# The last FFN block's output: residual rows written first, scaled result added by an accumulating scatter

## The chip, the cores and the metric

The kernel runs on one core of a Trainium2 chip. The metric is device time of one execution in microseconds (us). The engines named below are PE (TensorE, matmuls), DVE (VectorE), ACT (ScalarE), POOL (GpSimd, which also issues the indirect DMAs) and SP (SyncE, which issues the plain DMAs).

## What is computed

The reference, cut to what matters. `x` has 4 x 512 = 2048 tokens of 512 numbers; `L0_xattn_ref` sends each token through one of four gated products with the context of its expert, and `L0_ffn_ref` is a gated FFN with 1408 inner columns.

```python
def _L0_ffn_ref(x, gate_w, up_w, down_w, gate_s, up_s, down_s):
    g = jnp.einsum('th,ih->ti', xf, gate_w) * gate_s
    u = jnp.einsum('th,ih->ti', xf, up_w) * up_s
    hdn = jax.nn.silu(g) * u
    out = jnp.einsum('ti,hi->th', hdn, down_w) * down_s
...
x = x + jnp.tanh(g_xattn[0]) * _L0_xattn_ref(_layernorm(x, axis=-1), itok_BxS_13_99985, ctx_2048, ctx_2048, ctx_2048)
x = x + jnp.tanh(g_ffn[0]) * _L0_ffn_ref(_layernorm(x, axis=-1), L0_ffn_gate_w, L0_ffn_up_w, L0_ffn_down_w, L0_ffn_gate_s, L0_ffn_up_s, L0_ffn_down_s)
```

So each output row is x1 (the row after the first of these two updates) plus `tanh(g_ffn) * down_s` times the row of the down product.

## The kernel before, in words

The first part (up to about 170 us) sorts the tokens by expert, gathers their rows, computes the expert update and stores the updated rows x1 in a scratch tensor `x1_rows` in HBM (`x_rows` in the profile's names). The second part, `second_mlp`, is the FFN. It takes the 16 tiles of 128 tokens in four blocks (`b` = 0 to 3) of four tiles. In a block it goes through 11 chunks `c` of 128 inner columns: gate product and up product (L1032), SiLU on ACT (L511), product with the up part on DVE (L807), a split of the result into a high part (ACT, L515) and a low part (DVE, L812), and then the down product (L1045) into four PSUM banks `acc_ps[0..3]`, one for each tile `u` of the block. The down product of chunk c-1 runs behind the gate and up products of chunk c, and the last chunk of a block behind the first gate and up products of the next. For the last block nothing comes behind: its chunk 10 is cut in two halves of 256 columns (`halves`), and when it is done the program's last part begins.

A block is finished by `finish(b)` on DVE. For each pair of tiles it runs `scale` twice (L834: `tmp` or `xn` = `acc_ps[u]` times `dsb`, where `dsb` holds `tanh(g_ffn) * down_s`) and `add` twice (L841: `rows` = `rows` + `tmp` or `xn`, where `rows` holds x1). Each `add` raises the semaphore `rows_ready`. For blocks 0 to 2 it stands inside the next block's first chunk; `finish(3)` is the last thing on DVE.

POOL scatters each finished tile to `out` with an indirect DMA (L442), whose destination rows are in `oidx`. Tile u of PSUM is tile t = (u + 2) mod 4 of the block. In blocks 0 to 2 each scatter waits for the one before it to land (`out_stored`); the last four don't wait for each other and have a semaphore each (`last_stored[t]`). The order on every engine is the order of the program's text.

SP loads a block's x1 rows by two plain DMAs (`load_rows`, L304, semaphores `rows_a` and `rows_b`), for block 3 once eight scatters have landed. `rows` has eight slots of 512 numbers, four for each of two blocks. At the end SP waits for the four `last_stored` (L324), and each engine ends with a DRAIN and a semaphore exchange (L76, the end of the block of programs).

Of the kernel before, what the change touches and what calls it, by code (L numbers as in the profile page):

```python
# [18 lines left out]
ALU = mybir.AluOpType  # L19
# [11 lines left out]
STEPS = TILES + EXPERTS - 1  # L31
# [3 lines left out]
BLOCK = 4  # L35
BLOCKS = TILES // BLOCK
# [22 lines left out]
def row_slot(b, t):  # L59

    return (RING + BLOCK * b + t) % ROWS
# [7 lines left out]
def build(nc, x, ids, ctxT, g_x, g_f, guT, dwT, gate_s, up_s, down_s, out):  # L69
# [6 lines left out]
    with ExitStack() as ctx:  # L76
        def sb(name, shape, dt):
            return ctx.enter_context(nc.sbuf_tensor(name, shape, dt))
# [4 lines left out]
        def sem(name):  # L83
            return ctx.enter_context(nc.semaphore(name))
# [9 lines left out]
        rows = sb("rows", [P, ROWS, D], F32)  # L94
# [3 lines left out]
        dsb = sb("dsb", [P, D], F32)  # L98
# [15 lines left out]
        oidx = sb("oidx", [P, TILES], U32)  # L114
# [71 lines left out]
        acc_ps = bank[2:6]  # L186
# [40 lines left out]
        S = {n: sem(n) for n in names}  # L227
        ctx_landed = [sem(f"ctx_landed{e}") for e in range(EXPERTS)]
        down_landed = [sem(f"down_landed{n}") for n in range(4)]
        last_stored = [sem(f"last_stored{t}") for t in range(BLOCK)]  # L230

        def hold(eng):

            eng.sem_inc(S["held"])
# [92 lines left out]
        def _(pool):  # L327
# [32 lines left out]
            def inverse_std(m):  # L360
                pool.wait_ge(S["var_ready"], m + 1)
                pool.tensor_tensor(rstd[:, 0:1], ve[:, 0:1], half[:, :], ALU.pow)\  # L362
                    .then_inc(S["rstd_ready"], 1)
# [62 lines left out]

            pool.wait_ge(S["oidx_ready"], 1)

            for b in range(BLOCKS):
                if b + 1 < BLOCKS:  # L430
                    for t in range(BLOCK):
                        inverse_std(STEPS + BLOCK * (b + 1) + t)
                for u in range(BLOCK):
                    n, t = BLOCK * b + u, (u + 2) % BLOCK
                    pool.wait_ge(S["rows_ready"], STEPS + n + 1)
                    if b + 1 < BLOCKS:
                        if n:
                            pool.wait_ge(S["out_stored"], 16 * n)
                        done = S["out_stored"]
                    else:  # L440
                        done = last_stored[t]
                    pool.indirect_dma_start(  # L442
                        out, bass.IndirectOffsetOnAxis(ap=oidx[:, BLOCK * b + t:BLOCK * b + t + 1], axis=0),
                        rows[:, row_slot(b, t), :], None).then_inc(done, 16)

        @block.scalar
        def _(act):
# [86 lines left out]
        def _(dve):  # L534
# [292 lines left out]
            def scale(b, u):  # L827

                n = BLOCK * b + u
                buf = (tmp, xn)[u % 2]  # L830
                dve.wait_ge(S["acc_done"], n + 1)
                if u >= 2:
                    dve.wait_ge(S["rows_ready"], STEPS + n - 1)
                dve.tensor_tensor(buf[:, :].unsqueeze(1), acc_ps[u][:, :].unsqueeze(1),  # L834
                                  dsb[:, :].unsqueeze(1), ALU.mult).then_inc(S["scaled"], 1)

            def add(b, u):

                at = row_slot(b, (u + 2) % BLOCK)
                dve.wait_ge(S["scaled"], BLOCK * (b + 1) + u + 1)  # L840
                dve.tensor_tensor(rows[:, ds(at, 1), :], rows[:, ds(at, 1), :],  # L841
                                  (tmp, xn)[u % 2][:, :].unsqueeze(1), ALU.add)\
                   .then_inc(S["rows_ready"], 1)

            def finish(b):

                dve.wait_ge(S["dsb_ready"], 1)
                dve.wait_ge(S["rows_ready"], STEPS + BLOCK * b)
                for u in range(0, BLOCK, 2):
                    scale(b, u)  # L850
                    scale(b, u + 1)
                    add(b, u)
                    add(b, u + 1)

            def mlp_block(b, first=False, last=False):
                for c in range(IC):
                    chunk(b, c)
                    if first:
                        for d in range(3 * c, min(3 * c + 3, IC)):
                            down_lo(d)  # L860
                    if first and c == IC - 1:
                        dve.tensor_scalar(dsb[:, :], dsb[:, :], tg[:, 1:2], None, ALU.mult)\
                           .then_inc(S["dsb_ready"], 1)
                    if c == 0 and not first:
                        dve.wait_ge(S["xt_done"], STEPS + BLOCK * (b + 1))
                        finish(b - 1)
                    if c - 1 in PREP_AT and not last:
                        t = PREP_AT[c - 1]
                        x_lo(STEPS + BLOCK * (b + 1) + t, b + 1, (t + 2) % BLOCK)
                    if c in PREP_AT and not last:  # L870
                        if PREP_AT[c] == 0:
                            dve.wait_ge(S["rows_ready"], STEPS + BLOCK * b)
                        prepare(b + 1, PREP_AT[c])
# [4 lines left out]
            with dve.Fori(1, BLOCKS - 1) as b:  # L878
                mlp_block(b)
            mlp_block(BLOCKS - 1, last=True)  # L880
            finish(BLOCKS - 1)

        @block.tensor
        def _(pe):
# [225 lines left out]
```

## Time and profile before

| | us |
|---|---|
| median of 3 runs | 424.78 |
| lowest, highest | 424.2, 425.44 |
| span of the profiled execution (first to last instruction) | 422.8 |
| PE busy in the span | 373.6 (88%) |
| DVE busy | 249.7 (59%) |
| ACT busy | 139.7 (33%) |
| POOL busy | 98.6 (23%) |

The page's times are positions in the profiled span of 422.8 us, counted from its first instruction. The median of the runs, 424.78 us, is 2.0 us more than that span, which is what lies around the first and the last instruction. "L442" is a line of the kernel before. A name such as POOLq or DVEq is an engine's sequencer, which takes the waits, the DRAINs and the semaphore exchanges.

### The profile page before, as it was taken

How to read it: one execution, taken by the hardware profiler on the slowest of the kernel's cores; microseconds unless marked ns; L12 is line 12 of the kernel's file. 1: busy time of each engine (PE TensorE's matmuls, PEld its weight loads, DVE VectorE, ACT ScalarE, POOL GpSimd, SP SyncE). 2: the span in 40 equal slices, each digit the busy share in tenths (PEclk: the TensorE clock that was granted, in tenths of full speed). 3: DMA queues.
4: the chain of work that ended last, by engine and by line, in shares of the span. 5: the costliest groups of instructions: out<-in, count | busy, mean ns of one | idle time of the engine just before them, and what ended most of it. 6: DMA issues, size and time to landing. Idle time of an engine off the chain costs nothing.

```text
span 422.8 us, 6048 instructions
## 1 busy us (share of the span) xinstructions
PE 373.6 (88%) x1740; PEld 305.6 (72%) x1740; DVE 249.7 (59%) x461; ACT 139.7 (33%) x240; POOL 98.6 (23%) x135
## 2 busy tenths in 40 slices
PE   0117999999999984999999999999999999999990
PEld 0015788888778863888888888788888888888870
DVE  6998888888878782654653624654524645422243
ACT  4502545454545331542232222322222222222220
POOL 4553455554553221000000200100200100200003
PEclk9999999999999996999999999999999999999996
DMA  7445455655532043422000140000130000100002
GB/s 266 152 131 161 135 160 179 203 154 175 164 133 99 25 149 102 123 70 85 2 0 0 50 149 0 1 0 0 74 124 0 0 0 0 74 25 0 0 1 99
DMA packets 14956, 34.52 MB, mean 82 GB/s; under 512 B 2400, under 2 KB 2400, under 8 KB 14944
## 3 DMA queue, kind: packets, MB, share of 16 engines
q1 hardware_dynamic: 10624, 20.21, 15.1%
q0 software_dynamic: 4320, 14.16, 9.7%
q8 instruction: 6, 0.10, 0.1%
q14 instruction: 6, 0.05, 0.0%
HBM read 25.19 MB, written 9.18 MB: 81 GB/s over the span
## 4 chain that ended last, share of the span: by engine, by line
PE 84%; DVE 9%; issue 2%; POOL 2%; DMA 1%; POOLq 0%; ACT 0%; DVEq 0%
PE bank L1032 38%; PE bank L922 22%; PE bank L1045 19%; PE bank L914 3%; PE bank L936 2%; DVE work L239 1%; DMA rows<-x,gidx 1%; DVE shifted L625 1%; POOL out L442 1%; DVE work L677 1%; DVE is_low L607 1%; POOL rstd L362 1%; DVE is_low L633 1%; DMA ids_i<-ids 0%; DVE is_high L602 0%
## 5 line engine op out<-in xcount | busy, mean ns | idle before, releaser
L1032 PE MATMUL bank<-work,wgu 128*128 x704 | 169.4, 394 | 5.3 <-issue 5.3
L1032 PEld LDWEIGHTS bank<-work,wgu 128*128 128x128 f32 x704 | 133.9, 190 | 33.8 <-issue 5.5
L922 PE MATMUL bank<-work 128*128 x432 | 109.8, 403 | 3.6 <-DVE work L677 2.9
L922 PEld LDWEIGHTS bank<-work 128*128 128x128 f32 x432 | 79.7, 190 | 21.0 <-issue 5.2
L807 DVE SCALAR_TENSOR_TENSOR sh<-bank,gs,sh 128x512 f32<-128x512 f32 (+1 forms) x45 | 33.1, 738 | 96.9 <-PE bank L1032 96.8
L1045 PE MATMUL bank<-work,hp 128*128 128x512 f32 x352 | 88.2, 393 | 0.0
L1045 PEld LDWEIGHTS bank<-work,hp 128*128 128x128 f32 x352 | 65.1, 188 | 13.2 <-DVE hp L812 0.2
L511 ACT ACTIVATE sh<-bank,gs 128x512 f32<-128x512 f32 x44 | 30.3, 689 | 91.4 <-PE bank L1032 90.6
L515 ACT ACTIVATE hp<-sh 128x512 fp32r<-128x512 f32 (+1 forms) x45 | 28.0, 623 | 89.0 <-DVE sh L807 89.0
L362 POOL TENSOR_TENSOR rstd<-ve,half 128x1 f32<-128x1 f32 x31 | 17.9, 577 | 136.3 <-DVE ve L644 136.3
L812 DVE TENSOR_TENSOR hp<-sh,hp 128x512 fp32r<-128x512 f32 (+1 forms) x45 | 30.6, 681 | 30.1 <-ACT hp L515 30.0
L442 POOL DMA_INDIRECT out<-rows,oidx x16 | 16.3, 1022 | 117.6 <-DVE rows L841 94.0
L677 DVE TENSOR_TENSOR work<-bank,work 128x512 fp32r<-128x512 f32 (+1 forms) x35 | 23.8, 684 | 1.3 <-issue 1.0
L650 DVE TENSOR_SCALAR xn<-rows,mv,rstd 128x512 f32 (+1 forms) x31 | 16.9, 544 | 10.4 <-POOL rstd L362 10.4
L469 ACT ACTIVATE sh<-bank 128x512 f32<-128x512 f32 x19 | 11.4, 599 | 35.1 <-PE bank L922 35.1
L461 ACT ACTIVATE work<-bank 128x512 fp32r<-128x512 f32 (+1 forms) x35 | 20.4, 590 | 5.5 <-PE bank L904 3.8
L639 DVE BATCH_NORM_STATS2 bn<-rows 128x6 f32 (+1 forms) x31 | 21.2, 684 | 0.0
L914 PE MATMUL bank<-ident,xn 128*128 128x128 f32 x124 | 19.2, 278 | 2.0 <-issue 1.7
L914 PEld LDWEIGHTS bank<-ident,xn 128*128 128x128 f32 x124 | 15.3, 142 | 6.8 <-issue 2.4
L696 DVE SCALAR_TENSOR_TENSOR rows<-bank,tg,rows 128x512 f32 (+1 forms) x19 | 14.2, 749 | 8.3 <-PE bank L922 8.2
L703 DVE TENSOR_TENSOR wgu<-raw,wgu x16 | 14.3, 893 | 7.2 <-issue 7.2
L465 ACT ACTIVATE work<-bank 128x512 fp32r<-128x512 f32 x18 | 10.8, 600 | 18.1 <-PE bank L936 18.1
(125 smaller groups left out, 251.3 us busy)
## 6 DMA issues: line engine op xcount, KB each, us to landing
raw<-guT SPq DMA_DIRECT2D x16, 352.0 KB
ctx_in<-ctxT SPq DMA_DIRECT2D x4, 1024.0 KB, 9.1
rows<-x_rows SPq DMA_DIRECT2D x8, 512.0 KB, 4.2
checked<-dwT SPq DMA_DIRECT2D x11, 256.0 KB, 3.1
rows<-dwT SPq DMA_DIRECT2D x11, 256.0 KB, 2.7
dsb<-down_s SPq DMA_DIRECT2D x1, 256.0 KB, 5.2
out<-rows,oidx POOLq DMA_INDIRECT x16, 2.7
rows<-x,inow POOLq DMA_INDIRECT x12, 3.5
```

The source lines that it names most:

```text
L362: pool.tensor_tensor(rstd[:, 0:1], ve[:, 0:1], half[:, :], ALU.pow)\
L442: pool.indirect_dma_start(out, bass.IndirectOffsetOnAxis(ap=oidx[:, BLOCK * b + t:BLOCK * b + t + 1], axis=0), rows[:, row_slot(b, t), :], ...
L511: act.activation(sh[:, :], g_ps[:, :], ACT.Silu, scale=gs[:, 0, c:c + 1])\
L515: act.activation(hslot(c)[:, 0, part], sh[:, part], ACT.Copy)\
L639: dve.bn_stats(bn[:, 0, :], rows[:, ds(at, 1), :]).then_inc(S["bn_parts"], 1)
L677: dve.tensor_tensor(xpart(b, u, 1), turned[:, :], xpart(b, u, 0).bitcast(F32), ALU.subtract)\
L807: dve.scalar_tensor_tensor(out=sh[:, part], in0=u_ps[:, part], scalar=gs[:, 1, c:c + 1], in1=sh[:, part], op0=ALU.mult, op1=ALU.mult).then ...
L812: dve.tensor_tensor(hslot(c)[:, 1, part], sh[:, part], hslot(c)[:, 0, part].bitcast(F32), ALU.subtract)\
L914: mm = pe.transpose(xt_ps[:, c * P:(c + 1) * P], xn[:, c * P:(c + 1) * P], ident[:, :])
L922: mm = pe.matmul(out_ps[:, :], part(s)[:, c * P:(c + 1) * P], ctx_w(e, c, w), start=n == 0, stop=n == last)
L1032: mm = pe.matmul(out_ps[:, :], wgu[:, row + h, w, c * P:(c + 1) * P], moving, start=n == 0, stop=n == last)
L1045: mm = pe.matmul(acc_ps[u][:, :], hslot(c)[:, s, u * P:(u + 1) * P], down_w(c, w), start=c == 0 and n == 0, stop=c == IC - 1 and n == len( ...
```

## The change

For the last block alone, POOL now writes the block's x1 rows to `out` as soon as the block's x1 loads have landed and POOL is through with the scatters of block 2; each of these four scatters raises its own semaphore `x1_out[t]`. `finish(3)` is gone from DVE. In its place stand four multiplications of `acc_ps[u]` by `dsb`, which write straight into the slot of `rows` that held x1, after the scatter that reads that slot has landed (`x1_out[t]`). POOL then issues four scatters to the same rows of `out` with `compute_op=ALU.add`, each after the multiplication (`scaled`) and after the landing of the x1 row it adds to. Blocks 0 to 2 are as they were.

```diff
+        x1_out = [sem(f"x1_out{t}") for t in range(BLOCK)]
...
-            for b in range(BLOCKS):
-                if b + 1 < BLOCKS:
-                    for t in range(BLOCK):
-                        inverse_std(STEPS + BLOCK * (b + 1) + t)
+            def out_rows(b, t):
+                return bass.IndirectOffsetOnAxis(ap=oidx[:, BLOCK * b + t:BLOCK * b + t + 1], axis=0)
+
+            for b in range(BLOCKS - 1):
+                for t in range(BLOCK):
+                    inverse_std(STEPS + BLOCK * (b + 1) + t)
                 for u in range(BLOCK):
                     n, t = BLOCK * b + u, (u + 2) % BLOCK
                     pool.wait_ge(S["rows_ready"], STEPS + n + 1)
-                    if b + 1 < BLOCKS:
-                        if n:
-                            pool.wait_ge(S["out_stored"], 16 * n)
-                        done = S["out_stored"]
-                    else:
-                        done = last_stored[t]
-                    pool.indirect_dma_start(
-                        out, bass.IndirectOffsetOnAxis(ap=oidx[:, BLOCK * b + t:BLOCK * b + t + 1], axis=0),
-                        rows[:, row_slot(b, t), :], None).then_inc(done, 16)
+                    if n:
+                        pool.wait_ge(S["out_stored"], 16 * n)
+                    pool.indirect_dma_start(out, out_rows(b, t), rows[:, row_slot(b, t), :], None)\
+                        .then_inc(S["out_stored"], 16)
+
+            b = BLOCKS - 1
+            pool.wait_ge(S["rows_a"], 16 * BLOCKS)
+            pool.wait_ge(S["rows_b"], 16 * BLOCKS)
+            for t in range(BLOCK):
+                pool.indirect_dma_start(out, out_rows(b, t), rows[:, row_slot(b, t), :], None)\
+                    .then_inc(x1_out[t], 16)
+            for u in range(BLOCK):
+                t = (u + 2) % BLOCK
+                pool.wait_ge(S["scaled"], BLOCK * (b + 1) + u + 1)
+                pool.wait_ge(x1_out[t], 16)
+                pool.indirect_dma_start(out, out_rows(b, t), rows[:, row_slot(b, t), :], None,
+                                        compute_op=ALU.add).then_inc(last_stored[t], 16)
...
-            finish(BLOCKS - 1)
+
+            for u in range(BLOCK):
+                t = (u + 2) % BLOCK
+                dve.wait_ge(S["acc_done"], BLOCK * (BLOCKS - 1) + u + 1)
+                dve.wait_ge(x1_out[t], 16)
+                dve.tensor_tensor(rows[:, row_slot(BLOCKS - 1, t), :], acc_ps[u][:, :], dsb[:, :], ALU.mult)\
+                   .then_inc(S["scaled"], 1)
```

DVE at the very end of the program, before (numbers behind `bank` and `hp` are left out; L834 is `scale`, L841 is `add`):

```order
L812 TENSOR_TENSOR hp_51<-sh,hp_51 128x256 [waits hhi_ready] x2
L834 TENSOR_TENSOR tmp<-bank,dsb 128x512 [waits acc_done,rows_ready,dsb_ready]
L834 TENSOR_TENSOR xn<-bank,dsb 128x512 [waits acc_done]
L841 TENSOR_TENSOR rows<-rows,tmp 128x512 [waits scaled]
L841 TENSOR_TENSOR rows<-rows,xn 128x512 [waits scaled]
L834 TENSOR_TENSOR tmp<-bank,dsb 128x512 [waits rows_ready,acc_done]
L834 TENSOR_TENSOR xn<-bank,dsb 128x512 [waits rows_ready,acc_done]
L841 TENSOR_TENSOR rows<-rows,tmp 128x512 [waits scaled]
L841 TENSOR_TENSOR rows<-rows,xn 128x512 [waits scaled]
```

The same place after (L823 is the line that was L812):

```order
L823 TENSOR_TENSOR hp_51<-sh,hp_51 128x256 [waits hhi_ready] x2
L897 TENSOR_TENSOR rows<-bank,dsb 128x512 [waits x1_out2,acc_done]
L897 TENSOR_TENSOR rows<-bank,dsb 128x512 [waits x1_out3,acc_done]
L897 TENSOR_TENSOR rows<-bank,dsb 128x512 [waits x1_out0,acc_done]
L897 TENSOR_TENSOR rows<-bank,dsb 128x512 [waits x1_out1,acc_done]
```

Eight instructions became four, and the tile that is scattered first is written by the first of them instead of the third.

POOL at the end of the program, before, from the last `rstd` of block 3 on (the first four scatters are block 2's, the last four block 3's):

```order
L362 TENSOR_TENSOR rstd<-ve,half 128x1 [waits var_ready] x4
L442 DMA out<-rows,oidx 2048x512 [waits out_stored,rows_ready] x4
L442 DMA out<-rows,oidx 2048x512 [waits rows_ready] x4
L76 UNCONDITIONAL_BRANCH
```

The same place after:

```order
L363 TENSOR_TENSOR rstd<-ve,half 128x1 [waits var_ready] x4
L441 DMA out<-rows,oidx 2048x512 [waits out_stored,rows_ready] x4
L448 DMA out<-rows,oidx 2048x512 [waits rows_b,rows_a]
L448 DMA out<-rows,oidx 2048x512 x3
L454 DMA out<-rows,oidx 2048x512 [waits x1_out2,scaled]
L454 DMA out<-rows,oidx 2048x512 [waits x1_out3,scaled]
L454 DMA out<-rows,oidx 2048x512 [waits x1_out0,scaled]
L454 DMA out<-rows,oidx 2048x512 [waits x1_out1,scaled]
L76 UNCONDITIONAL_BRANCH
```

Four scatters (L448) were put between block 2's and the last four, and the last four (L454) are of the accumulating kind and wait for two things each.

## Rows read from the trace of the kernel before

**Rows 1.** The page: busy tenths of PE, granted clock, by slices of 10.6 us

```profile
PE   0117999999999984999999999999999999999990
...
PEclk9999999999999996999999999999999999999996
```

**Rows 2.** Chain that ended last, in order of time: start, us, what

```profile
411.01 0.69 DVE tmp L834
411.70 0.60 DVE xn L834
412.30 0.61 DVE rows L841
412.91 0.27 issue
413.18 1.16 POOL out L442
414.33 0.30 issue
...
416.86 1.26 POOLq L76
```

**Rows 3.** Timeline of the end: start, us, engine, line, what, idle before

```profile
411.62 0.68 DVE L834 TENSOR_TENSOR xn<-bank,dsb 128x512 f32<-128x512 f32 x1
412.22 0.68 DVE L841 TENSOR_TENSOR rows<-rows,tmp 128x512 f32<-128x512 f32 x1
...
415.29 0.68 DVE L841 TENSOR_TENSOR rows<-rows,xn 128x512 f32<-128x512 f32 x1
...
417.17 0.96 POOL L442 DMA_INDIRECT out<-rows,oidx  x1 [0.30 <-issue]
```

**Rows 4.** Line L76, the program's end, by engine: duration in ns, start

```profile
L76 POOLq DRAIN  x1: 6609/6609/6609, 416.0 to 416.0; - x1
L76 SPq DRAIN  x1: 7/7/7, 420.2 to 420.2; - x1
L76 SPq EVENT_SEMAPHORE  x1: 17/17/17, 422.8 to 422.8; - x1
...
L76 DVEq DRAIN  x1: 1270/1270/1270, 414.7 to 414.7; - x1
```

**Rows 5.** Line L442, the last four scatters (from 400 us on): ns, landing

```profile
L442 POOL DMA_INDIRECT out<-rows,oidx x4: 956/960/1159, 413.2 to 417.2; - x4
...
DMA to landing us min/median/max: 2.7/2.7/2.9
```

**Rows 6.** DMA queues, 412 to 423 us, in 40 slices of 0.275 us: busy tenths

```profile
DMA  0000000000599009950399108970000000000000
...
q0 software_dynamic: 320, 1.05, 25.0%
```

**Rows 7.** Line L351, the gathers from HBM by POOL: ns, landing

```profile
L351 POOL DMA_INDIRECT rows<-x,inow x12: 1013/1023/1030, 53.6 to 125.8; - x12
...
DMA to landing us min/median/max: 3.3/3.6/5.3
```

**Rows 8.** Timeline around block 2's scatters and behind them

```profile
366.62 0.69 DVE L812 TENSOR_TENSOR hp<-sh,hp 128x512 fp32r<-128x512 f32 x1 [0.70 <-ACT hp L515]
...
369.23 0.96 POOL L442 DMA_INDIRECT out<-rows,oidx  x1 [2.53 <-DMA out<-rows,oidx]
...
372.07 0.69 DVE L812 TENSOR_TENSOR hp<-sh,hp 128x512 fp32r<-128x512 f32 x1 [0.70 <-ACT hp L515]
```

**Rows 9.** Busy time by stretch: us, PE, PEld, DVE, ACT, POOL, clock, DMA

```profile
358.00:372.00 14.00, 14.00 (x64) 11.58 (x63) 6.78 (x11) 3.79 (x6) 4.10 (x4) 1.00 0.20 75
372.00:382.00 10.00, 10.00 (x46) 8.29 (x45) 2.64 (x4) 2.05 (x4) 0.00 (x0) 1.00 0.00 0
```

**Rows 10.** Timeline of SP from 300 us on: block 3's x1 loads

```profile
310.11 0.87 SPq L304 DMA_DIRECT2D rows<-x_rows  x2
```

## The prediction

> **What bounds the kernel now.** I read the page's busy tenths first: PE is at 9 in nearly every slice from the fifth to the last but one, at full granted clock but for one slice ahead of the FFN (around 165 us) [rows 1]. So during the FFN blocks anything that DVE, POOL or the DMA engines do beside PE is free as long as PE gets its operands in time, and only the last slice is open to this change. Then the chain of waits in order of time [rows 2]: up to 411.0 us it is matmuls; from there it runs over two `scale` on DVE, one `add`, 0.27 us of semaphore and start, and then POOL's four scatters back to back. After that the timeline of the same stretch [rows 3] and the program's end by engine [rows 4].
>
> The end has two stretches. The first is DVE from the last accumulation to the first row ready for POOL: 411.01 to 412.91, three steps of 0.60 to 0.69 us. The second is POOL: its first scatter starts at 413.18 and takes 1.16 us, the others 0.96 with 0.30 between them, so the last starts at 417.17 and ends at 418.13 [rows 2, 3, 5]. DVE is through with its last `add` at 415.97 [rows 3], 1.2 us before POOL takes that tile: **from the first scatter on, POOL's issue rate sets the pace, not DVE**. The data follow: each scatter shows as a burst of about 3 slices of 0.275 us with gaps between the bursts, and the last burst ends near 419.4 [rows 6]; landed is 2.7 us after the start of the issue, 419.87 [rows 3, 5]. SP is released then and is at its own DRAIN at 420.2. But the span ends at 422.8, and what ends just before is POOL's DRAIN: 416.0 + 6.61 = 422.6 [rows 4]. That is 4.5 us after POOL's last issue and 2.7 us after the last landing; the DVE's DRAIN, 414.7 + 1.27 = 415.97, ends exactly with its last instruction [rows 3, 4]. **What POOL's DRAIN waits for, the issue or the landing, this trace doesn't tell**, since there is one such DRAIN in it. That is the choice on which the forecast hangs most.
>
> **The change part by part.**
>
> *Four x1 scatters on POOL, early.* They stand behind block 2's last scatter, which ends at 370.19 [rows 8]. Their waits on `rows_a` and `rows_b` are long met: SP issued block 3's loads at 310.1 to 311.0 [rows 10]. So they run from about 370.5 on, 4 x 0.96 + 0.2 + 3 x 0.30 = 4.9 us, to about 375.5, and land by 378. Nothing stands behind them on POOL until 411.7, and SP waits only for the last four. The work that hides them is PE's: between 358 and 372 us PE was busy 14.00 of 14.00 us with four such scatters beside it (4.10 us of POOL, DMA share 0.20), as it was between 372 and 382 without any [rows 9]. DVE's `hp` subtraction took 0.69 us beside and without a scatter [rows 8]. Cost: 0. If the cover were not there they would cost 4.9 us of POOL, which is why they have to be before 411.
>
> *DVE's new waits on `x1_out`.* They are met 33 us before `acc_done`. Queued behind them are only the four multiplications themselves. Cost: one more semaphore check, under 0.05 us on the first.
>
> *DVE's `add` gone.* The row that POOL takes first is ready when the first multiplication ends. Before, that took two `scale` and one `add` (0.69 + 0.60 + 0.61 us); now it takes one instruction of 0.69 us, ending at 411.70. The gain is 412.91 - 411.70 = **1.21 us** on the chain. The other three follow at 0.60 us each (412.3, 412.9, 413.5), faster than POOL takes them, so the four further instructions that fall away bring nothing. POOL's first scatter starts at 411.70 + 0.27 + 0.01 = 411.98 instead of 413.18.
>
> *The accumulating scatter, issue.* No row shows one. Its nearest row is the plain scatter of the same tile, 0.96 us [rows 5], and that is the lower end: the same 128 indices and the same two tensors. An upper end is twice that, 1.92, if reading the old row of `out` costs POOL as much again as the whole plain issue. Between them the plain gather with 1.02 us [rows 7] shows how far POOL's indirect issues spread by form. I take 1.02, near the plain row, because the list of indices is read once either way, and add nothing for the second wait, which is met when its turn comes. Then the last issue ends at 411.98 + 0.20 (the first one's excess) + 4 x 1.02 + 3 x 0.30 = 417.16, against 418.13: **-0.97 us**. At 0.96 it is -1.20, at 1.44 (half as much again) it is 418.84, or +0.7, at 1.92 it is +2.6. The two break even at 1.26 us an issue.
>
> *The accumulating scatter, data.* It reads the tile, reads the old rows of `out` and writes them. The plain one has the DMA engines for about 0.69 us (a quarter of 11 us for four, [rows 6]) of the 1.27 us between issues; twice that, 1.4 us, is a little more than the interval, and would queue 0.1 us on each. The read also comes ahead of the write in time. Gathers from HBM landed after 3.3 to 5.3 us, scatters after 2.7 [rows 5, 7]. With 0.6 to 2.6 us more than 2.7, the last landing is 411.98 + 0.20 + 3 x 1.32 + 3.3 to 5.3 = 419.4 to 421.4, against 419.87. I take the lower third of it, 419.9, since the gathers' 5.3 was beside other traffic and here there is none: the shift of 0.97 is eaten, and **the last row lands when it does now**. SP has 2.6 us from its DRAIN to the end of the span [rows 4], so up to about 422 this is hidden, if POOL's DRAIN doesn't wait for it.
>
> The page "Collectives: The Full Stack" of the Trainium skill (The bandwidth ceiling) speaks against this part: a reduce in the DMA engines needs two source reads for each chunk, both on one ring, and runs at half the rate of a copy. By it the scatter's 0.69 us would be 1.4, which the sum above has already as its bound; nothing in this case's trace shows an accumulating DMA to agree or differ.
>
> *Sum.* Issue -0.97, landing hidden: span 422.8 - 0.97 = 421.8, and with the 2.0 us around it 423.8.
>
> **The rivals.**
>
> A, the forecast: POOL's DRAIN follows its last issue by 4.5 us. 423.8, from 423.6 (0.96 us an issue) to 424.3 (1.15).
>
> B, the gain is handed back by the landing: POOL's DRAIN waits until the DMAs have landed and adds its 2.7 us. Then the end moves with the landing, 419.4 to 421.4 against 419.87: -0.5 to +1.5, likeliest near 0 to +0.3: 424.9. For it: the DRAIN is the only one that outlasts its engine's last instruction, and only POOL has DMAs of this kind out. Against it: 2.7 us after a landing is long for an engine that is merely told of it, when SP gets from its wait to its DRAIN in 0.3.
>
> C, the other side: accumulating issues are dearer than POOL's pace allows. The chain is POOL's four issues, so each extra 0.1 us costs 0.4. The place is the last 6 us; it is slower than now from 1.26 us an issue, and by over 1.27 us (0.3%) from 1.58. At 1.44 it gives 425.5. For it: three addresses a row instead of two. Against it: gathers and scatters of different form lie within 0.06 us of each other.
>
> D, the DMA engines add slowly: three times the copy's 0.69 us and more. Then the bursts join, 4 x 2.1 us from the first data at about 413.5, the last row lands at about 422.3 and SP's part ends the span near 422.8 if the DRAIN doesn't wait (424.8), or near 425.2 if it does (427.2).
>
> **How the numbers follow.** Chances: A 0.45, B 0.26, C 0.18, D 0.11. The likeliest is A, so the predicted time is 423.8. The range takes in A and B whole and C up to 1.6 us an issue, and leaves out D with the DRAIN waiting and a dearer C: 423.2 to 426.2, which also allows for the 0.5 us by which single runs stand apart. A measurement of this kernel tells about 0.3%, 1.27 us, from no change; faster by that means below 423.51, which A reaches only at its lower end and with luck: 0.14. Slower by that means above 426.05: half of D, a third of C, a quarter of B: 0.05 + 0.07 + 0.07, and a little for what I have not thought of: 0.22. The rest, 0.64, is within 0.3%.
>
> **What would show each step.** In the profile after: the first multiplication at 411.0 and the first accumulating scatter at 412.0 (if later, the waits on `x1_out` cost). The duration of the last four scatters: about 1.0 us is A or B, 1.3 or more is C. Four plain scatters near 370.5 to 375.5 with PE still fully busy in 372 to 382. Time to landing of the last four: 2.7 to 3.7 is the sum, above 5 with bursts that touch each other is D. The end of POOL's DRAIN against the last issue and the last landing: 4.5 us after the issue is A, 2.7 after the landing B. The prediction fails if the issue or the landing of an accumulating scatter lies outside the bounds taken, or if DRAIN has a cost of its own with such DMAs.

## The result and the profile after

The changed kernel takes 427.86 us (median of 4 runs, 427.26 to 427.92) against 424.49 us for the kernel before beside it: ratio 1.0073, 95% interval 1.0059 to 1.0087. By the ratio it is 3.1 us slower, where 1 us less was forecast, and it lies outside the range of 423.2 to 426.2. The profiled execution has a span of 425.7 us, 2.9 more than before.

Line numbers of the changed kernel: L897 is the last multiplication on DVE, L448 the early scatter, L454 the accumulating scatter, L1062 the down product. Up to the end of PE's work nothing differs. This is busy time by stretch, with the columns of [rows 9], for the changed kernel:

```profile
358.00:372.00 14.00, 14.00 (x63) 11.59 (x63) 6.72 (x11) 3.76 (x6) 5.37 (x6) 1.00 0.20 77
372.00:382.00 10.00, 10.00 (x46) 8.29 (x45) 2.70 (x4) 2.01 (x3) 2.57 (x3) 1.00 0.27 102
```

PE is as full as in [rows 9] with the four early scatters beside it. The end, from the timeline of the changed kernel, answers to [rows 2, 3]:

```profile
410.86 2.48 DVE L897 TENSOR_TENSOR rows<-bank,dsb 128x512 f32<-128x512 f32 x4 [0.45 <-PE bank L1062]
411.83 1.60 POOL L454 DMA_INDIRECT out<-rows,oidx  x1 [36.65 <-DVE rows L897]
413.73 1.58 POOL L454 DMA_INDIRECT out<-rows,oidx  x1 [0.30 <-issue]
...
417.48 1.55 POOL L454 DMA_INDIRECT out<-rows,oidx  x1 [0.31 <-issue]
```

POOL starts 1.35 us earlier than before (411.83 against 413.18); 0.15 of it is PE, which ended that much earlier in this execution, and 1.20 is the change, as the sum had it. But each issue takes 1.57 us instead of 0.96, so the last one ends at 419.03 instead of 418.13. The lines of the accumulating scatter (L454), of the DMA queues from 412 to 426 us in 40 slices of 0.35 us, and of the program's end (L76) answer to [rows 5], [rows 6] and [rows 4]:

```profile
L454 POOL DMA_INDIRECT out<-rows,oidx x4: 1551/1568/1597, 411.8 to 417.5; - x4
...
DMA to landing us min/median/max: 5.0/5.4/5.6
```

```profile
DMA  0000099959699899998999998996200000000000
...
q0 software_dynamic: 576, 1.05, 56.3%
```

```profile
L76 POOLq DRAIN  x1: 12082/12082/12082, 413.4 to 413.4; - x1
...
L76 SPq DRAIN  x1: 7/7/7, 423.4 to 423.4; - x1
```

Landing takes 5.0 to 5.6 us instead of 2.7. The bursts that stood apart in [rows 6] have run together, from 413.8 to about 422. The same 1.05 MB went in 576 packets instead of 320, and the DMA engines were busy for 0.563 x 14 = 7.9 us, 1.97 a scatter, instead of 0.69. The last row lands at 423.1, SP is at its DRAIN at 423.4, and POOL's DRAIN ends at 413.4 + 12.1 = 425.5, 2.4 us after the last landing and 6.5 after POOL's last issue. Before, it was 2.7 and 4.5. Neither of the two distances that the forecast chose between was kept, so what that DRAIN does had to be found out.

### The profile page after: what moved, and what is told of

The parts are those of the page before. It is cut to its first block, busy times and chain, and to the rows that moved or that the text cites. A ratio compares the mean times of both kernels' runs of the same rounds, so it can differ in the third digit from the quotient of the medians.

```text
span 425.7 us, 6054 instructions
## 1 busy us (share of the span) xinstructions
PE 374.5 (88%) x1740; PEld 306.8 (72%) x1740; DVE 247.5 (58%) x457; ACT 139.6 (33%) x240; POOL 104.5 (25%) x139
## 4 chain that ended last, share of the span: by engine, by line
PE 72%; issue 12%; DVE 9%; DMA 3%; POOL 2%; ACT 1%; POOLq 0%; DVEq 0%
PE bank L1049 30%; PE bank L939 23%; PE bank L1062 14%; PE bank L931 3%; DMA out<-rows,oidx 3%; PE bank L953 2%; DVE work L240 1%; DVE shifted L636 1%; POOL out L454 1%; DVE work L688 1%; DVE is_low L618 1%; DVE is_low L644 1%; POOL out L448 0%; POOLq L76 0%; DMA ids_i<-ids 0%
## 5 line engine op out<-in xcount | busy, mean ns | idle before, releaser
L1062 PE MATMUL bank<-work,hp 128*128 128x512 f32 x352 | 88.2, 393 | 0.0
L1062 PEld LDWEIGHTS bank<-work,hp 128*128 128x128 f32 x352 | 65.1, 188 | 13.2 <-DVE hp L823 0.2
L823 DVE TENSOR_TENSOR hp<-sh,hp 128x512 fp32r<-128x512 f32 (+1 forms) x45 | 30.6, 680 | 30.1 <-ACT hp L526 30.0
L441 POOL DMA_INDIRECT out<-rows,oidx x12 | 12.3, 1025 | 73.7 <-DVE rows L852 51.0
L476 ACT ACTIVATE work<-bank 128x512 fp32r<-128x512 f32 x18 | 10.8, 599 | 17.9 <-PE bank L953 17.9
```

Source lines behind the costliest of these rows:

```text
L823: dve.tensor_tensor(hslot(c)[:, 1, part], sh[:, part], hslot(c)[:, 0, part].bitcast(F32), ALU.subtract)\
L1062: mm = pe.matmul(acc_ps[u][:, :], hslot(c)[:, s, u * P:(u + 1) * P], down_w(c, w), start=c == 0 and n == 0, stop=c == IC - 1 and n == len( ...
```

## The experiments

All are timed beside the kernel before. The ratio given is the one that its interval belongs to; the quotient of the two medians differs from it by up to 0.1%. The start of the tail moves by up to 1.5 us between profiled executions (the first multiplication lies at 409.9 to 411.4 us), so positions at the end are compared by their distances, not as they stand.

One thing has to be kept in mind for the comparisons with the kernel before. Its second plain scatter starts within 0.05 us of a DVE `add`. In the profiled executions of the kernel before and of e10_drain_mid its issue took 0.96 us, in those of e2_early, e3_pool_tail, e5_early_acc and e9_twelve_early 1.48 to 1.49 (the rows are in the last section). So 0.53 us of the end can come or go without any of the edits; how often it does in the runs that were only timed isn't known.

**e1_plain: the changed kernel without the adding.** The last four scatters overwrite the x1 rows, so this kernel leaves out the x1 term in the last block.

```diff
-                pool.indirect_dma_start(out, out_rows(b, t), rows[:, row_slot(b, t), :], None,
-                                        compute_op=ALU.add).then_inc(last_stored[t], 16)
+                pool.indirect_dma_start(out, out_rows(b, t), rows[:, row_slot(b, t), :], None)\
+                    .then_inc(last_stored[t], 16)
```

> The changed kernel with compute_op=ALU.add taken from the last four scatters: they overwrite the x1 rows with the scaled result instead of adding to them, so this kernel leaves out the x1 term in the last block's rows. Everything else of the change stays (early x1 scatters, four multiplications, waits). Theory 1 (the loss lies in the accumulating scatters alone: 1.57 us an issue instead of 0.96, 1.9 us of the DMA engines instead of 0.68, landing after 5.4 us instead of 2.7): the rest of the change is worth what the sum gave, -1.2 us against the kernel before, so about 423.3 us, ratio 0.997. Rival (the early scatters or the new waits cost something that the profile hides): 424.5 us or more. The last four issues take 0.96 us in theory 1.

Measured: 423.14 us against 424.83, ratio 0.9962 (0.9946 to 0.9978). The line of its last four scatters:

```profile
L454 POOL DMA_INDIRECT out<-rows,oidx x4: 957/960/961, 412.1 to 415.9; - x4
...
DMA to landing us min/median/max: 2.7/2.7/2.7
```

With `compute_op` gone the issue is back at 0.96 and the landing at 2.7. So both prices belong to the accumulating scatter. The rest of the change brings 1.6 us by the ratio, 0.9 to 2.3 by the interval, and 1.0 in the profiled execution from the first multiplication to the end of the span (421.9 - 411.13 = 10.8, before 422.8 - 411.01 = 11.8). The forecast 1.2 lies within. The 1.0 is made up of 1.2 for the earlier start, 0.2 for the first issue, which took 0.96 instead of 1.16, and 0.3 lost behind the last issue: POOL's DRAIN ends 4.8 us after it instead of 4.5. The accumulating form costs the difference between this and the changed kernel, 1.1% or some 4 to 5 us.

**e2_early and e5_early_acc: the early scatters alone.** Both are the kernel before with four scatters of block 3's x1 rows behind block 2's, and the last four waiting for them. In e5_early_acc the early ones are accumulating and wait for each other; what they add is overwritten by the last four.

```diff
+                if b == BLOCKS - 1:
...
+                    for t in range(BLOCK):
+                        pool.indirect_dma_start(
+                            out, bass.IndirectOffsetOnAxis(ap=oidx[:, BLOCK * b + t:BLOCK * b + t + 1], axis=0),
+                            rows[:, row_slot(b, t), :], None).then_inc(x1_out[t], 16)
...
```

> The kernel before with the four early x1 scatters alone added (plain, behind block 2's scatters; the last four wait for them, the final add stays on DVE). Theory 1: no difference, ratio 1.000 within 0.2%, PE fully busy in 372 to 382 us. Rival (extra DMA traffic and POOL work beside PE costs): 0.5 to 1.5 us more.

> As e2_early, but the four early scatters are accumulating ones, each waiting for the one before it to land; what they add is overwritten by the last four. Measures an accumulating scatter by itself, beside PE and off the path. Issue 1.57 us each. If its landing of 5.0 to 5.6 us in the changed kernel was its own (reading and adding), it is about 5.0 here too; if it was queueing behind its neighbours, nearer to 3.5. Time of the kernel: as before, 424.5, since all is over by about 395 us.

Measured: e2_early 1.0013 (1.0000 to 1.0026), e5_early_acc 1.0021 (1.0008 to 1.0034). PE is full in both. The first is on the edge of no difference, the second some 0.9 us slower although its early scatters are over 20 us before the end; its end resembles e2_early's, and the two intervals overlap. From the first multiplication to the end of the span e2_early's profiled execution takes 0.86 us more than that of the kernel before (12.69 against 11.83): 0.53 of it is the second issue's 1.49 us, and 0.33 a longer distance from POOL's last issue to the end of its DRAIN. The line of the early accumulating scatters of e5_early_acc, one at a time beside PE:

```profile
L441 POOL DMA_INDIRECT out<-rows,oidx x4: 1962/2005/2046, 371.5 to 387.9; - x4
...
DMA to landing us min/median/max: 5.1/5.2/5.3
```

So most of the slow landing is an accumulating scatter's own, 5.1 to 5.3 us with no neighbour; e4_acc_first has 4.5 and e8_acc_last 4.8. These figures count from the start of the issue, and here the issue took 2.0 us, since each began 0.10 to 0.16 us after a DVE subtraction of two SBUF tiles (last section). From the end of the issue it is 2.9 to 3.4 us for the ones without an accumulating neighbour (e4_acc_first, e8_acc_last and e5_early_acc) and 3.4, 3.8, 3.8 and 4.0 for the changed kernel's four. So some 0.6 to 1.1 us of the last one's landing come from its neighbours. About 0.3 of it is queueing that the rows account for (1.97 us of data at intervals of 1.88 us, three times over); the rest stays open.

**e3_pool_tail: 2.1 us more of POOL work behind the last scatter, in the kernel before.**

```diff
+            for tile in (tmp, xn, sh):
+                pool.memset(tile[:, :], 0.0)
+            pool.memset(raw[:, RAWS - 1, :], 0.0)
```

> The kernel before with about 2.4 us of memsets on POOL (three tiles of 512 and one of 704 columns) put behind its last scatter, where nobody waits for them. They end near 420.5 us, after the last landing (419.9) and before the end of POOL's DRAIN now (422.6). If the DRAIN follows POOL's last instruction by a fixed 4.5 us (forecast A): the end moves by 2.4 us to about 426.9, ratio 1.0055. If it is tied to the landing of the DMAs (rival B): no change, 424.5, ratio 1.000.

Measured: 427.0 us, ratio 1.0049 (1.0034 to 1.0065), which is the 2.1 us that the memsets took (2.4 had been planned), as a DRAIN that follows POOL's last instruction expects. The end in its timeline:

```profile
418.12 0.96 POOL L442 DMA_INDIRECT out<-rows,oidx  x1 [0.30 <-issue]
...
420.47 0.70 POOL L447 MEMSET raw<- 128x704 f32 x1
```

And the end of its program (L76):

```profile
L76 POOLq DRAIN  x1: 9291/9291/9291, 416.4 to 416.4; - x1
```

The last memset ends at 421.17, the DRAIN at 425.7: 4.5 us again, though the last row had landed at 420.8. So in the kernel before, too, it isn't the landing that sets the end.

**e7_after_tail: the same memsets behind the changed kernel's last scatter.** The edit is the one above.

> The changed kernel whole, with 2.4 us of memsets on POOL behind its last accumulating scatter, as in e3. POOL's last instruction ends near 421.4 instead of 419.0. If the DRAIN behind accumulating scatters follows POOL's last instruction by a fixed 6.45 us: +2.4 us on the changed kernel, about 430.3, ratio to the kernel before 1.013. If it is the later of two, 4.5 to 4.9 us after POOL's last instruction and 2.4 us after the last landing (423.1): the landing had set the end, and only 0.5 to 0.8 us are added, about 428.5, ratio 1.009.

Measured: 427.97 us, ratio 1.0074 (1.0056 to 1.0092), no slower than the changed kernel within the interval; a fixed distance behind POOL's last instruction would have given 430.3. The last memset in its timeline, and then its line L76:

```profile
419.96 1.28 POOL L458 MEMSET raw<- 128x704 f32 x1
```

The program's end:

```profile
L76 POOLq DRAIN  x1: 12207/12207/12207, 413.8 to 413.8; - x1
```

POOL ends at 421.24 instead of 419.03, the DRAIN at 426.0 instead of 425.5. It now comes 4.8 us after POOL's last instruction. So 1.7 of the 2.2 us were hidden: in the changed kernel the DRAIN's end is set by the landing, and its issues alone would have given 419.03 + 4.8 = 423.8.

**e8_acc_last and e4_acc_first: one accumulating scatter.** In e8_acc_last only the last of the four tiles is added by the scatter, in e4_acc_first only the first; the other three go through DVE's `add` (in e4_acc_first in the order scale, add). From the diff of e8_acc_last, POOL's part:

```diff
...
+                    if n == TILES - 1:
+                        pool.wait_ge(x1_out, 16)
+                        pool.indirect_dma_start(
+                            out, bass.IndirectOffsetOnAxis(ap=oidx[:, BLOCK * b + t:BLOCK * b + t + 1], axis=0),
+                            rows[:, row_slot(b, t), :], None, compute_op=ALU.add).then_inc(done, 16)
+                        continue
...
```

> The kernel before with only the last tile added by an accumulating scatter (its x1 rows written early); three plain issues in front as before. The last issue starts at 417.2, takes 1.6 us to 418.8, and lands 5.2 us after its start, 422.4. If the end follows the issue by 4.5 to 4.9 us: 423.3 to 423.7, +0.7 to +1.1 us, about 425.5, ratio 1.002. If it follows the landing by 2.4 us: 424.8, +2.0 us, about 426.7, ratio 1.005.

> The changed kernel with only the first tile of the last block added by an accumulating scatter (and written early); the other three go as in the kernel before, scale, add, plain scatter, in turn. POOL starts at 412.0 instead of 413.2, takes 1.57 us and then three times 0.96: the last issue starts near 416.4 against 417.17. The accumulating scatter's slow landing (5.2 us, so 417.2) lies beside the other issues. Both theories of the end (DRAIN after the last issue, or after the last landing) expect -0.5 to -0.8 us: 424.0 to 424.3 us, ratio 0.9985. If each accumulating scatter makes the DRAIN longer by its own (0.4 us each in the changed kernel), 0.4 us less of a gain.

Measured: e8_acc_last 1.0032 (1.0017 to 1.0047), e4_acc_first 0.9989 (0.9973 to 1.0005). In e8_acc_last the DRAIN ends 2.3 us after the last landing and 5.5 after the issue. Its timeline has the issue:

```profile
416.98 1.60 POOL L450 DMA_INDIRECT out<-rows,oidx  x1 [0.30 <-issue]
```

and its line L76 the end:

```profile
L76 POOLq DRAIN  x1: 8897/8897/8897, 415.2 to 415.2; - x1
...
L76 SPq COMPARE_BRANCH  x1: 43/43/43, 422.0 to 422.0; - x1
```

The last landing releases SP just ahead of that branch, at 421.8; the DRAIN ends at 424.1. The landing sets the end, and one slow scatter in the last place is enough to lose. In the first place its landing is covered by the three issues behind it. Its issue is 0.44 us longer than the kernel before's first, and the issue behind it took 1.32 us instead of 0.96, beside a DVE `add` that had begun 0.23 us ahead of it; together that is less than the 1.2 us by which POOL starts earlier. The gain isn't clear of the interval.

**e6_in_turn: no new kind of DMA, only the order of the last finish.** This is the kernel before with `finish(BLOCKS - 1, in_turn=True)`:

```diff
...
+                if in_turn:
+                    for u in range(BLOCK):
+                        scale(b, u)
+                        add(b, u)
+                    return
...
```

> The kernel before, with no accumulating and no early scatter; only the order in the last finish on DVE is changed: scale, add, scale, add, so that the first tile is ready after two instructions instead of three. The first scatter starts 0.5 us earlier, POOL's issues set the pace of the rest, and the DRAIN follows the last one by 4.5 us: -0.5 us, 424.3 us, ratio 0.999. Rival: the add waits for its own scale's result and the pair takes longer than 1.4 us, so nothing is gained.

Measured: 423.75 us, ratio 0.9986 (0.9973 to 0.9998). DVE, from its timeline:

```profile
410.21 0.69 DVE L834 TENSOR_TENSOR tmp<-bank,dsb 128x512 f32<-128x512 f32 x1 [0.55 <-PE bank L1050]
410.94 0.69 DVE L841 TENSOR_TENSOR rows<-rows,tmp 128x512 f32<-128x512 f32 x1
```

An `add` directly behind its own `scale` starts 0.73 us after it, where instructions that don't wait for each other start 0.60 apart. So the first row is ready 1.42 us after the start of the first `scale` (411.63) instead of 1.90. POOL's last issue comes 0.5 us nearer to the first multiplication (6.64 against 7.12 us), and the ratio says 0.6 us, 0.1 to 1.1 by the interval. So some 0.5 us of the changed kernel's aim of 1.2 is had without touching a DMA.

**e9_twelve_early: does the DRAIN count DMAs?** Up to here the distance from POOL's last instruction to the end of its DRAIN, where the landing didn't set it, was 4.5 us in before, e3, e6 (54 indirect DMAs in all) and e4 (55), and 4.8 in e1, e2, e5 and e7 (58). 4.5 / 54 = 0.083, and 58 x 0.083 = 4.8. This kernel is e2_early with its four scatters three times over, 66 in all.

```diff
...
-                    for t in range(BLOCK):
+                    for i in range(3 * BLOCK):
+                        t = i % BLOCK
+                        if i >= BLOCK:
+                            pool.wait_ge(x1_out[t], 16 * (i // BLOCK))
...
```

> e2_early with twelve early x1 scatters instead of four (the same rows three times), all beside PE. So far POOL's DRAIN ended 4.48 to 4.55 us after POOL's last instruction in kernels with 54 or 55 indirect DMAs in all, and 4.76 to 4.86 us in kernels with 58. Theory 3: the DRAIN costs about 0.083 us for each indirect DMA that POOL has issued in the whole program (54 x 0.083 = 4.5, 58 x 0.083 = 4.8); with 66 it is 5.5 us, and the kernel some 1.0 us slower than before, 425.8. Rival: a fixed 4.5 us with an accident of 0.3: 4.5 to 4.9 us again and 425.0 to 425.4.

Measured: 1.0024 (1.0009 to 1.0039). Its last issue, from the timeline:

```profile
417.78 0.96 POOL L456 DMA_INDIRECT out<-rows,oidx  x1 [0.30 <-issue]
```

Its program's end (L76):

```profile
L76 POOLq DRAIN  x1: 8187/8187/8187, 416.0 to 416.0; - x1
```

418.74 to 424.2 is 5.5 us, what 66 x 0.083 gives. The time alone wouldn't show it, since the second issue took 1.49 us here as well: of the 1.5 us more than before in the profiled execution, 0.53 is that issue and 1.0 the DRAIN.

**e10_drain_mid, e11_drain_in_turn and e12_after_drain: an early DRAIN.** One DRAIN more on POOL near 371 us, when all scatters of block 2 have landed and POOL has nothing to do: in the kernel before, in e6_in_turn, and in the changed kernel. The edit in the first two:

```diff
+                if b == BLOCKS - 1:
+                    pool.wait_ge(S["out_stored"], 16 * BLOCK * b)
+                    pool.drain()
```

> The kernel before with one DRAIN more on POOL, behind block 2's last scatter and after all twelve have landed (near 372 us), where POOL has nothing else to do for 40 us. Theory 3 (a DRAIN works off each indirect DMA since the last one): the early one takes 50 x 0.083 = 4.2 us beside PE, and the one at the end has four left, 0.3 us. The end is then set by the last landing (419.9) and what the DRAIN or SP adds to it: 0.5 us in the best case, span 420.4, 2.4 us less than before, ratio 0.9945; 2.35 us, as behind the accumulating scatters, in the worst, span 422.4, 0.4 us less. Rival (4.5 us fixed): no change, ratio 1.000.

> e10_drain_mid and e6_in_turn together: the early DRAIN on POOL and the order scale, add, scale, add in the last finish. If both gains add up: e10's and another 0.5 us; best case ratio 0.993 (421.7 us). If the DRAIN costs 4.5 us whatever stands before it: as e6, 0.9986.

> The changed kernel whole with an early DRAIN on POOL behind block 2's scatters. If the 2.4 us between the last landing (423.1) and the end of the DRAIN in the changed kernel are work for each indirect DMA of the program, they fall to 0.5 us or less: span near 423.7, still 0.9 us more than before, ratio 1.002. If they are a fixed answer time after a landing: no change on the changed kernel, 427.9, ratio 1.0075.

Measured: e10_drain_mid 422.16 us, ratio 0.9951 (0.9933 to 0.9968); e11_drain_in_turn 421.29 us, 0.9931 (0.9913 to 0.9949); e12_after_drain 425.37 us, 1.0026 (1.0012 to 1.0040). The line of the early DRAIN of e10_drain_mid (L435):

```profile
L435 POOLq DRAIN  x1: 4154/4154/4154, 371.2 to 371.2; - x1
```

Its last issue, from the timeline:

```profile
416.46 0.96 POOL L445 DMA_INDIRECT out<-rows,oidx  x1 [0.30 <-issue]
```

And its line L76:

```profile
L76 POOLq DRAIN  x1: 4072/4072/4072, 415.3 to 415.3; - x1
...
L76 SPq DRAIN  x1: 7/7/7, 419.5 to 419.5; - x1
```

50 indirect DMAs stand before the early DRAIN, nothing is in flight, and it takes 4.154 us: **0.083 us for each**. At the end the DRAIN is over at 419.4, 2.0 us after POOL's last issue and 0.2 after the last landing, and the span ends at 419.7. The work on those 50 has gone behind PE; the gain at the end is 2.4 us by the distances and 2.1 by the ratio, since now the landing is what sets the end. Line L76 of e12_after_drain shows the same for accumulating scatters:

```profile
L76 POOLq DRAIN  x1: 9939/9939/9939, 413.0 to 413.0; - x1
...
L76 SPq COMPARE_BRANCH  x1: 43/43/43, 422.7 to 422.7; - x1
```

The last row now lands at 422.5 and the DRAIN ends 0.4 us behind it, at 422.9. Between e10_drain_mid and e12_after_drain, where the landing alone ends both, the change costs 3.2 us (425.37 against 422.16). e11_drain_in_turn is the fastest of the kernels measured here, ahead of both the kernel before and the changed one.

## Why the prediction was wrong

By its own steps:

- *Early x1 scatters, cost 0.* Right for PE and the path in the middle (14.00 of 14.00 and 10.00 of 10.00 us). Wrong for the end: four more indirect DMAs put the end of POOL's last DRAIN 0.33 us further behind its last issue (4.82 instead of 4.49). The cost was looked for only where the scatters run. e2_early measured 0.13% more (0.00 to 0.26), and the second issue's 0.53 us can be in that too.
- *DVE's new waits, under 0.05 us.* No run shows a price of such a wait. DVE idled 0.45 us ahead of the first multiplication, against 0.53 ahead of the first `scale` before, so none is to be seen.
- *DVE's `add` gone, -1.21.* Right: from the first multiplication to the first scatter it is 0.97 us instead of 2.17, and e1_plain gained 1.6 us in all, with the forecast inside its interval. The sum kept the first issue's 0.20 us of excess; behind a multiplication that excess is gone.
- *Issue of an accumulating scatter, 1.02 us.* The value was wrong, the bounds of 0.96 and 1.92 weren't: 1.57 us. The argument for the value, that the list of indices is read once either way, leaned on gathers and scatters, which only copy each row; nothing of that kind could show what adding to the old one costs. Why it costs 0.6 us of issue stays open. Four issues took 6.29 us instead of 4.04, +2.25, and with the -1.35 the last issue ended 0.90 us later than before.
- *Data and landing.* This failed worst. The DMA engines' time was bounded by twice the copy's 0.69 us and was 1.97, close to the 2.1 us of rival D; the forecast of 419.9 for the last row puts its landing at 3.8 us (the last issue would start at 416.14) and it was 5.6, above even the 5.3 of the gathers, which was put aside for having had other traffic beside it.
- *What POOL's DRAIN waits for.* It was put as a choice between the last issue and the last landing. It is both, and a third thing: it needs 0.083 us for each indirect DMA since the last DRAIN (its list, for short), and it doesn't end before the last landing. With plain scatters and no early DRAIN the first sets the end (A's 4.5 us), with an accumulating one in last place the second does (B's mechanism).
- *The combination.* B, C and D were given chances as if one excluded the others. C and D hold, and so does B's mechanism once the landing is late, and they add: against before, the last issue ends 0.90 us later, the DRAIN's list is 0.33 longer, and the landing holds the DRAIN 1.7 beyond that (e7_after_tail), which is the span's 2.9. The upper end of 426.2 took in no two of them together; D with the DRAIN waiting was priced at 427.2 and left out. (D's own terms, 413.5 + 4 x 2.1, give 421.9 for the last row, where 422.3 was written.)

The 2.3 to 2.4 us between landing and the end of the DRAIN (changed kernel and e8_acc_last) fall to 0.4 when the list has been worked off early (e12_after_drain). So they are list work that couldn't be done before the landing; why that share and not all of the 4.8 us stays open.

## What to carry to other kernels

A DMA form that the trace has never shown should be measured by itself before it goes on the last few microseconds of a kernel; off the path its landing costs nothing, in last place all of it counts. Look at what an engine does after its last useful instruction: a DRAIN that outlasts it is work, and here a second DRAIN placed where GpSimd idles was worth more (0.5%) than the whole aim of the change. And rivals that can hold at the same time are terms of a sum, not cases.

## What the runs showed of the hardware

- GpSimd's DRAIN takes 0.083 us for each indirect DMA that GpSimd has issued since its last DRAIN, even if they have long landed: 4.15 us for 50 with none in flight (e10_drain_mid), and from GpSimd's last instruction on 4.5 for 54, 4.8 for 58, 5.5 for 66.
- An accumulating scatter of 128 rows of 2 KB: issue 1.55 to 1.60 us (2.0 in e5_early_acc, where it began beside a DVE subtraction), 144 packets, 2.0 us of the 16 DMA engines, with neighbours (1.97) or without (2.0 to 2.1 in e5_early_acc), landing 4.5 us (e4_acc_first, in front of plain ones) to 5.6 us. The plain one: 0.96 us, 80 packets, 0.69 us, 2.7 us. The Trainium skill ("Collectives: The Full Stack", The bandwidth ceiling) has such a reduction at half a copy's rate, since it reads two sources, and not slowed by the adding itself; by it 1.4 us is the estimate. The trace doesn't agree: it has 2.9 times the copy's 0.69, and no run tells where the rest goes.
- A plain issue took 1.49 us instead of 0.96 where it began 0.03 us after a DVE `add`. From the timeline of e2_early:

```profile
413.53 0.68 DVE L852 TENSOR_TENSOR rows<-rows,tmp 128x512 f32<-128x512 f32 x1
413.56 1.49 POOL L453 DMA_INDIRECT out<-rows,oidx  x1 [0.30 <-issue]
```

  In the kernel before the same pair stood 0.02 us apart, and there it was the `add` that took longer:

```profile
414.62 0.74 DVE L841 TENSOR_TENSOR rows<-rows,tmp 128x512 f32<-128x512 f32 x1
414.64 0.96 POOL L442 DMA_INDIRECT out<-rows,oidx  x1 [0.30 <-issue]
```

  Accumulating scatters show it too. This is the first of e5_early_acc, whose issue takes 2.0 us instead of 1.6:

```profile
371.40 0.69 DVE L825 TENSOR_TENSOR hp<-sh,hp 128x512 fp32r<-128x512 f32 x1 [0.70 <-ACT hp L528]
371.54 2.03 POOL L441 DMA_INDIRECT out<-rows,oidx  x1 [2.02 <-DMA out<-rows,oidx]
```

  The size follows from what is left of the DVE instruction when the issue begins, less 0.12 us: 0.65 left gave 0.53 more (e2_early, e3_pool_tail, e9_twelve_early), 0.46 gave 0.36 (e4_acc_first), 0.33 gave 0.20 (the first of the last four in the kernel before, its 1.16 us), 0.19 gave 0.06 (e8_acc_last). DVE's multiplications of a PSUM bank by an SBUF tile lengthen no issue (0.96 for e1_plain's first two, 1.60 for the changed kernel's first, as for e8_acc_last's with DVE idle). That fits an exclusive use of a shared port by whichever comes first, which is what the Trainium skill says of DVE instructions with two SBUF inputs beside a GpSimd one that reads SBUF ("SBUF — State Buffer", SBUF: two separate sides). It says so of the whole instruction. The traces agree for DVE's instruction, not for the issue: a subtraction that began 0.3 to 0.9 us into an issue took its usual 0.69. Which of the two goes first can't be told from starts 0.02 us apart, for in e9_twelve_early that distance went to the `add`. No run here was made to separate this.
